# A recommendation tower in one program: VectorE's work planned in pieces of five rows, twenty weighted rows moved to TensorE, and the first label slabs loaded later

## What is computed

```
x[b,n,:]  = tbl_n[ids[b,n]]                          # 1024 x 50 x 300
score     = exp((x @ w_a + b_a) @ w_b), PAD where x's row is all zero (sum of |x|)
q1, q2    = sum_n softmax(score)[n] * x[:,n,:]       # two heads
h         = concat(q1, q2) @ w5 + b5                 # 300
f6        = h @ w6 + b6
f7        = (h[iu] * h[ju] * g) @ w7 + b7            # all 44,850 pairs i < j; g = (v @ v.T)[iu,ju]
out8      = concat(f6, f7) @ w8 + b8
z[b,k]    = out8[b] . label_embedding[b,k,:]         # 200 labels: 240,000 bytes an example
y         = relu(relu(concat(z, dense_ctx) @ W1 + b1) @ W2 + b2) @ W3
```

## Time and profile before

| | |
|---|---|
| median of 3 runs | 1859.72 us (1857.41 to 1860.12) |
| profiled execution | 1857.68 us, its span 1855.9 us |
| share of the span busy: TensorE, its weight loads, VectorE | 91%, 67%, 90% |
| ScalarE, GpSimd | 56%, 30% |
| TensorE clock over the span | 0.964 of full |
| DMA | 561.70 MB, mean 303 GB/s |

### The profile page before, as it was taken

One profiled execution on the slowest core, in us unless ns is written; L12 is line 12 of the kernel. 1 busy time (PEld: TensorE's weight loads), 2 busy tenths in 40 slices (PEclk: granted clock), 3 DMA queues, 4 the chain that ended last, 5 costly groups with the idle time before them and its releaser, 6 DMA issues.

```text
span 1855.9 us, 26051 instructions
## 1 busy us (share of the span) xinstructions
PE 1688.6 (91%) x7084; PEld 1249.4 (67%) x7084; DVE 1674.5 (90%) x5836; ACT 1030.0 (56%) x3233; POOL 549.8 (30%) x413
## 2 busy tenths in 40 slices
PE   2788899999999999999999999999997999997851
PEld 1555567777777777777776777777775777775531
DVE  5998989989999889999999999899997888967785
ACT  3786684674466644456654764455753544454534
POOL 7774707827300124400087018500000000000053
PEclk8899999999999999999999999999998999999975
DMA  9488955748978688989769666998649999989985
GB/s 277 112 280 296 350 189 191 236 168 294 372 300 325 227 336 341 358 325 347 288 219 345 254 253 212 393 384 310 252 162 386 411 377 369 402 333 419 419 351 242
DMA packets 97949, 561.70 MB, mean 303 GB/s; under 512 B 16591, under 2 KB 16837, under 8 KB 72205
## 3 DMA queue, kind: packets, MB, share of 16 engines
q1 hardware_dynamic: 78525, 498.39, 69.8%
q0 software_dynamic: 19264, 61.64, 10.7%
q10 hardware_dynamic: 16, 0.00, 0.0%
HBM read 559.98 MB, written 0.00 MB: 302 GB/s over the span
## 4 chain that ended last, share of the span: by engine, by line
PE 47%; DVE 29%; DMA 10%; POOL 6%; issue 5%; ACT 2%; SPq 0%; DVEq 0%; ACTq 0%; POOLq 0%
PE acc L986 40%; DVE junk L609 13%; DVE qa L651 9%; DVE prod L761 7%; DMA w_sb<-in_w 7%; POOL x L555 4%; DMA lab<-in_labels 3%; PE coarse L836 2%; POOL lab L555 1%; PE acc L901 1%; PE misc L908 1%; PE acc L883 1%; PE acc L886 1%; ACT heads L1106 1%; ACT x L1116 1%
## 5 line engine op out<-in xcount | busy, mean ns | idle before, releaser
L986 PE MATMUL acc<-w_sb,prod 128*128 128x300 f32 (+2 forms) x5648 | 1528.4, 421 | 60.9 <-DMA w_sb<-in_w 37.1
L986 PEld LDWEIGHTS acc<-w_sb,prod 128*128 128x128 f32 (+2 forms) x5648 | 1044.1, 192 | 406.7 <-issue 49.0
L1211 ACT ACTIVATE prod<-prod,g_all 128x256 f32<-128x256 f32 (+4 forms) x1615 | 686.7, 470 | 493.2 <-DVE prod L761 491.1
L555 POOL DMA_INDIRECT x<-in_tbl,ids_sb x376 | 479.8, 1276 | 676.7 <-DVE qa L651 569.4
L761 DVE TENSOR_TENSOR prod<-fine,coarse 128x1280 f32<-128x1280 f32 (+4 forms) x325 | 422.5, 1304 | 88.0 <-PE coarse L836 87.2
L609 DVE SCALAR_TENSOR_TENSOR junk<-lab,out 128x300 f32<-128x300 f32 x1056 | 424.7, 465 | 22.4 <-DMA lab<-in_labels 22.1
L609 DVE SCALAR_TENSOR_TENSOR junk<-x,score_u 128x300 f32<-128x300 f32 x752 | 303.6, 466 | 20.5 <-DMA x<-in_tbl,ids_sb 20.5
L651 DVE SCALAR_TENSOR_TENSOR qa<-x,ex,qa 128x300 f32<-128x300 f32 x628 | 282.5, 519 | 0.0
L586 POOL TENSOR_TENSOR x<-x,out 128x2400 f32<-128x2400 f32 x6 | 31.6, 5265 | 598.0 <-ACT out L1081 589.3
L1106 ACT ACTIVATE heads<-x 128x300 f32<-128x300 f32 x376 | 152.5, 406 | 26.3 <-DMA x<-in_tbl,ids_sb 24.7
L609 DVE SCALAR_TENSOR_TENSOR junk<-x,out 128x300 f32<-128x300 f32 x344 | 137.6, 466 | 0.0
(11 more groups left out here) (114 smaller groups left out, 616.2 us busy)
## 6 DMA issues: line engine op xcount, KB each, us to landing
w_sb<-in_w SPq DMA_DIRECT2D x320, 750.0 KB, 6.5
lab<-in_labels SPq DMA_DIRECT2D x140, 1200.0 KB, 7.9
x<-in_labels SPq DMA_DIRECT2D x60, 1200.0 KB, 8.9
x<-in_tbl,ids_sb POOLq DMA_INDIRECT x376, 5.5
w_sb<-in_w SPq DMA_DIRECT2D x5, 450.0 KB, 4.3
prod<-in_v_i SPq DMA_DIRECT2D x1, 710.0 KB, 4.5
prod<-in_v_j SPq DMA_DIRECT2D x1, 710.0 KB, 7.3
w_sb<-in_w SPq DMA_DIRECT2D x1, 703.1 KB
```

The lines of the kernel that those rows point to most:

```text
L555: pool.indirect_dma_start(out=row_of(t, n), out_offset=None, in_=tables[n], in_offset=bass.IndirectOffsetOnAxis(ap=ids_sb[:, t, n:n + 1], ...
L986: last = pe.matmul(acc[:, t % 3, 0:EMB], prod[0:rows, u % RING, m, t % 2 * P:(t % 2 + 1) * P], w7_sb[0:rows, u % W7_RING, m * EMB:(m + 1) ...
L1211: act.activation(chunk, chunk, ACT.Copy, scale=g_all[0:rows, pair:pair + 1]).then_inc(chunk_ready, 1)
```

## The change

1. VectorE's dots and weighted sums are planned in pieces of 5 rows instead of 10 (`PIECE`, `PIECES`), each at about half the price (20 and 22 instead of 40 and 45).
2. A product is due 0.6 us (one tile) or 2.6 us (two tiles) after the product two before it; before, 0.45 of the unit's price: 1.3 and 2.565 us.
3. The first 10 fields of tile 1 are weighed by TensorE: 20 diagonals on ScalarE (`diag_for_pe`, one a tick from the unit after `normalise`), 20 matmuls on TensorE (`weigh_by_pe`, one a tick from the unit after that) into `acc[:, 1:3]`; VectorE has 80 rows of weighted sums for that tile instead of 100, and one more sum in `pooled`. Waits are added for the diagonals' space (before `fine`'s third buffer is written) and for the two parts of the sums; the loads of the first label slabs and the gathers of tile 2 count TensorE's fields too.
4. The first three label slabs stand before w7 block 60 in SyncE's queue; before, they stood after block 36.

```diff
+PIECE = FG
+PIECES = 2 * HALVES
+PE_FIELDS = 10
+PE1 = 2 * PE_FIELDS
+DVE1 = 2 * FIELDS - PE1
...
-COST = {"dots": 40, "wsums": 45, "slab": 32, "mask": 15, "normalise": 8, "pooled": 9}
+COST = {"dots": 20, "wsums": 22, "slab": 32, "mask": 15, "normalise": 8, "pooled": 9}
+DUE = (0, 6, 26)
+FIRST_SLABS = 60
...
-            due = FIRST_CROSS if c < 2 else begun[c - 2] + 0.45 * UNIT[len(active(c - 2))]
+            due = FIRST_CROSS if c < 2 else begun[c - 2] + DUE[len(active(c - 2))]
...
+    loads = [load[1:] for load in sorted(loads, key=lambda load: load[0])]
+    early = [("slab", n) for n in range(SLOTS)]
+    loads = [load for load in loads if load not in early]
+    at = loads.index(("w7", FIRST_SLABS))
+    return before, items, tail, pool_ticks, loads[:at] + early + loads[at:], switch
...
+NORMALISED = next(u for u in range(TOTAL) if ("normalise", 1, 0) in ITEMS[u])
+DIAG_TICK = (NORMALISED + 1) * FINE
+PE_TICK = DIAG_TICK + FINE
...
             def pooled(t):
...
+                if t == 1:
+                    dve.wait_ge(diag_used, sum(PE0) + PE1)
+                    dve.tensor_tensor(qa[:, 0], qa[:, 0], acc[:, 1:3, 0:EMB], ALU.add).then_inc(first_sums, 1)
...
+            def weigh_by_pe(i):
+                n, head = i // 2, i % 2
+                k = sum(PE0) + i
+                pe.wait_ge(diag_ready, k + 1)
+                pe.matmul(acc[:, 1 + head, 0:EMB], diag[:, k % DIAGS, :], row_of(1, n),
+                          start=i < 2, stop=i >= PE1 - 2).then_inc(diag_used, 1)
...
+                    if 0 <= u * FINE + m - PE_TICK < PE1:
+                        weigh_by_pe(u * FINE + m - PE_TICK)
...
+            def diag_for_pe(i):
+                if i == 0:
+                    act.wait_ge(chain, CHAIN0 + CHAIN)
+                n, head = i // 2, i % 2
+                k = sum(PE0) + i
+                act.wait_ge(diag_used, k - DIAGS + 1)
+                act.activation(diag[:, k % DIAGS, :], ident[:], ACT.Copy,
+                               scale=ex[:, head, n:n + 1]).then_inc(diag_ready, 1)
```

More of the change, by code:

```diff
@@ L163, in plan @@
     pool_ticks, loads = {}, [(0, "w7", u) for u in range(W7_RING)]
-    dots = [("dots", t, h) for t in range(1, TILES) for h in range(HALVES)]
+    dots = [("dots", t, h) for t in range(1, TILES) for h in range(PIECES)]
     rest = [item for t in range(1, TILES) for item in
-            [("mask", t, 0), ("normalise", t, 0)] + [("wsums", t, h) for h in range(HALVES)] + [("pooled", t, 0)]]
+            [("mask", t, 0), ("normalise", t, 0)] + [("wsums", t, h) for h in range(PE1 // PIECE if t == 1 else 0, PIECES)]
+            + [("pooled", t, 0)]]
     slabs = [("slab", t, s) for t in range(TILES) for s in range(SLABS)]
@@ L206, in plan @@
         if dots and dots[0][1] <= rest[0][1] + 1:
-            when = landed.get(dots[0][1:], 1e9)
+            when = landed.get((dots[0][1], dots[0][2] // 2), 1e9)
             if dots[0][1] == rest[0][1] or at > now and when <= now:
@@ L240, in plan @@
             dots.pop(0)
-            for n in range(h * FG, (h + 1) * FG):
+            for n in range(h // 2 * FG, (h // 2 + 1) * FG) if h % 2 else ():
                 if t > 1 or n >= HEAD_ABS:
@@ L271 @@
 assert all((kind, t * SLABS + s) != ("slab", n) for n in BY_POOL for u in ITEMS for kind, t, s in u)
-ROWS_OF = {"dots": HALF, "slab": SLAB}
+ROWS_OF = {"dots": PIECE, "slab": SLAB}
 ROWS_BEFORE, _rows = {}, JUNK
-for _item in [("dots", 0, h) for h in range(HALVES)] + BEFORE + [i for u in ITEMS for i in u] + TAIL:
+for _item in [("dots", 0, h) for h in range(PIECES)] + BEFORE + [i for u in ITEMS for i in u] + TAIL:
     ROWS_BEFORE[_item] = _rows
@@ L610, in row, with dots @@
                                          accum_out=out).then_inc(rows_done, 1)
-            def dots(t, half):
-                dve.wait_ge(gathered[t % 2][half], gathers(t))
-                for i in range(HALF):
-                    n, head = (half * HALF + i) // 2, i % 2
-                    row(ROWS_BEFORE["dots", t, half] + i, row_of(t, n), score_u[:, head, 0:EMB],
+            def dots(t, piece):
+                dve.wait_ge(gathered[t % 2][piece // 2], gathers(t))
+                for i in range(PIECE):
+                    n, head = divmod(piece * PIECE + i, 2)
+                    row(ROWS_BEFORE["dots", t, piece] + i, row_of(t, n), score_u[:, head, 0:EMB],
                         score[:, t % 2, head, n:n + 1])
@@ L652, in weigh, with wsums @@
                                              ALU.mult, ALU.add).then_inc(wsum_done, 1)
-            def wsums(t, half):
-                for k in range(half * HALF, (half + 1) * HALF):
+            def wsums(t, piece):
+                for k in range(piece * PIECE, (piece + 1) * PIECE):
                     weigh(t, k, k // 2, k % 2, qa[:, k // 2 % 2, k % 2, :])
@@ L796, in _ @@
             for half in range(HALVES):
-                dots(0, half)
+                dots(0, 2 * half)
+                dots(0, 2 * half + 1)
                 if half == 2:
@@ L1050, in copy_fine @@
                 ms = range(2 * n, min(2 * n + 2, shifts_of(u)))
+                if part_count(u) == PLACES - 1:
+                    act.wait_ge(diag_used, sum(PE0) + PE1)
                 made = misc[0:rows, 0:len(ms) * 2 * P].rearrange("p (m b) -> p m b", b=2 * P)
@@ L1119, in exp_scores @@
             def exp_scores(t, fields=range(FIELDS)):
[L1120 removed]
+                act.wait_ge(rows_done, ROWS_BEFORE["dots", t, 2 * (fields[-1] // FG) + 1] + PIECE)
                 for head in range(2):
```

28 lines of the change are left out of this document (17 added, 11 removed).

## The result

The changed kernel takes 1863.01 us (median of 12 runs, 1859.47 to 1866.23) against 1858.97 us of the kernel before (12 runs, 1855.95 to 1864.49) on the same chips. The ratio is **1.0025, 95% interval 1.0015 to 1.0036**: slower, by a little more than can be told from no change, where 13 us less were forecast. The profiled execution has a span of 1861.7 us, 5.8 more than the 1855.9 of before.

What follows compares the result with a forecast made beforehand. No single engine was taken to bound the kernel; the limit changes by stretch, with transfers deciding late. First solo stretch -8, two-tile stretch 0, second solo stretch and end -5 sum to -13 us: 1847 us, range 1835 to 1861.

Steps and rivals of the forecast that it cites:

- Units 0 to 17, 54 us: First solo stretch, its start: w7 transfers beside the gathers, 3.0 us a block, are slowest of four engines: 54 us.
- Rival 3: Units 0 to 17: w7 blocks come too slowly, 3.5 us each beside the gathers, 63 us; kernel 1853 us; chance 0.15.
- Units 18 to 21, 12.5: First solo stretch: mask, normalising, ten dots and five weighted rows beside four products on VectorE take 12.5 us.
- units 22 to 25, 20.8: First solo stretch: TensorE's 20 weighing matmuls add 10.3 us to its four units, 20.8 us in all.
- Units 26 to 33, 26.2: First solo stretch: 23.1 us, plus 3 of TensorE waiting for the last 20 weighted rows before product 34: 26.2 us.
- Units 34 to 40, 27: End of the first solo stretch: 27 us against 32.8 before, without the w7 wait and with ten abs fewer.
- The slab loads cost nothing and take the 4.1 us wait away: First three label slabs, moved behind w7 block 59: cost nothing, 8.8 us at most, and end a 4.1 us w7 wait.
- Two-tile stretch 0, bounds -4 to +6: Middle of the kernel: no change, bounds -4 to +6 us; the 9.7 us w7 wait stays, one unit later.
- Second solo stretch -6 (+3 for the later start of tile 6, -8.8 for three slabs fewer): From 1628.5 us: tile 6 starts later, +3; three slabs fewer share the DMA engines, -8.8; last product 6 us sooner.
- Behind it +9.4 for 24 rows, 4.3 of it in the gap, so -5 in all: After the last product: 24 more tile 6 rows, +9.4 us, 4.3 filling idle time; with the second solo stretch, -5.
- Rival 2: End: the last product is not sooner, so three lagging slabs cost VectorE +9.4 us; 1861 us; chance 0.15.
- Rival 1: First solo stretch: TensorE is as full as its busy time says, so 20 matmuls add 10.3 us; 1865 us; chance 0.10.

Runs made afterwards that it cites:

- old_due: The changed kernel with the planner's product due times set back to those of the kernel before: 1854.17 us, ratio 0.9980 to the kernel before.
- no_pe_fields: The changed kernel without TensorE's 20 weighing matmuls, VectorE weighing all 50 fields of the second tile: 1861.8 us, ratio 1.0019 to the kernel before.
- both repairs: The changed kernel with tile 6's rows behind the last product reading one operand from PSUM, and tile 1's 20 weighted rows before product 34 moved earlier: 1844.21 us.
- tile7_sbuf: The changed kernel without the copy to PSUM, so tile 7's rows read two SBUF operands beside GpSimd's products: 1890.32 us, ratio 1.0172 to the kernel before.

## Why the prediction was wrong, by its own steps

- *Units 0 to 17, 54 us.* Right: 52.8, and the DMA share 0.92 at 340 GB/s there. Rival 3 (slow blocks) is out. Of the 14.3 us less than before, two thirds are VectorE's work that moved behind unit 17 (old_due above).
- *Units 18 to 21, 12.5; units 22 to 25, 20.8.* Right: 12.7 and 20.8. TensorE's matmuls cost nearly their full 10.3 us (20.8 against 10.8 in no_pe_fields).
- *Units 26 to 33, 26.2.* Measured 28.2, and **the wait before unit 34 mis-sized**: 3 forecast, 7.12 measured. The heap is longer by the pooling's 0.78 + 0.78 us, and product 34 (0.8) and its first chunk on ScalarE (0.6) come behind it: 8.91 + 1.56 + 0.8 + 0.6 = 11.9 us from 202.81. The cover was what TensorE had left from there, to 207.66: 4.85 us, near the 5.3 of the text. So it was the heap's length that was short, by the 3 us chained behind its rows; and 9.0 - 5.3 is 3.7, not 3.
- *Units 34 to 40, 27.* Measured 28.8, and 25.8 with the heap spread: the lower clock after that wait is a term the sum did not have. The first stretch as a whole: -8 forecast, -3.8 measured, -12.9 with the heap spread (134.2).
- *The slab loads cost nothing and take the 4.1 us wait away.* The wait is gone, and in the kernel before that is worth 7 us; but in the changed kernel the heap would have covered these loads where they stood, so moving them brought nothing.
- *Two-tile stretch 0, bounds -4 to +6.* Measured +4.8, inside; it is products that come late (5.8 us more of waiting for ScalarE), and with the old plan from unit 34 it is -2.8. The 9.7 us wait was to stay: it is one of 5.7 at unit 248 and one of 4.6 at unit 181 now.
- *Second solo stretch -6 (+3 for the later start of tile 6, -8.8 for three slabs fewer).* The size is right, -7.1, and the reason is not: the stretch moves the same 56.7 MB. That is luck. With the -8 of the start the last product was to come some 14 us sooner; it came 5.9 sooner (1773.0 to 1767.1).
- *Behind it +9.4 for 24 rows, 4.3 of it in the gap, so -5 in all.* This is **the step that failed**. By the text it was to grow by 5.1 us if VectorE decides and by 1 us as the transfers do, which were taken to count; it grew by 11.7. The rows were priced at 0.39 us each from rows of the kernel before, where tile 6's ran alone and tile 7's had an operand in PSUM, and GpSimd's start, which the earlier last product pulls forward, was not followed onto VectorE. The earlier trace rows showed VectorE waiting 4.3 us between tile 6's rows and the copy of tile 7's; that gap was also the distance between the two engines, and filling it was counted as free. With the meeting taken away the end takes 86.6 us, +3.7 on before, against the +5.1 of the text.
- *Rival 2* (the lagging slabs come due on VectorE, 1861) had the place, but not the mechanism: its condition, that the last product is not sooner, did not hold. *Rival 1* (1865), the one on the slower side, is out: units 0 to 17 come each 2.9 us and not 3.6, and the stretch did not grow. Both times lie 2 us from the measured one, and neither for its reason. Of the signs of being wrong that were named, the last one came: the rows behind the last product ended the kernel later than the transfers allow (DMA share 0.17 in 1780 to 1790).

By stretches, the forecast was off by 4.2 us in the first, 4.8 in the middle, 1.1 the other way in the second solo stretch and 10.7 at the end, 18.6 in all, and 8.0 of them are the meeting (94.6 against 86.6). With both repairs the kernel takes 1844.2 us against 1847.0 forecast, but that nearness is in part luck, too: its first stretch is 5.6 us better than the forecast (133.5 against 147.1 - 8), its middle 3.8 and its end 4.1 worse. What was missing was an interaction that no row of the kernel before shows, though the code hints at it: a copy of one row into PSUM for tile 7 alone.

The profile after shows the loss as work: VectorE is "busy" for 64.88 of 67 us. The Trainium skill (SBUF — State Buffer, Who interferes with whom) says that a VectorE instruction with two SBUF inputs contends with a GpSimd instruction that reads SBUF, that the port pair they share is an exclusive lock, and that the order of issue decides which of the two blocks. The runs agree: eight long rows of 5.5 us for eight products in tile7_sbuf, and none with the operand in PSUM. They show who waits and for how long; that a port is what the two share, no run here shows. Had the prediction used that sentence, one more rival would have been: two products of 5.3 us beside 48 rows, 5.0 us for each by estimate, so +10 us and 1857 instead of 1847.
